# The attention output's column tiles hold token quarters in place of heads, and VectorE's block transposes replace TensorE's turns

## The chip, the cores and the metric

The kernel runs on one NeuronCore of a Trainium2 chip. The metric is the device time of one execution in microseconds (us), the median over the runs. Engines are named as in the profile: PE is TensorE's matmuls and PEld its weight loads, DVE is VectorE, ACT is ScalarE, POOL is GpSimd, and SP is SyncE, which here issues the DMAs.

## The reference

Two conditional attention layers follow each other on x of 8 sequences x 512 tokens x 512 features, all in float32. Only the second matters for the change; its core is:

```python
xn = layer_norm(x, norm_w, norm_b)
q = (xn @ q_w + q_b).reshape(Bx, Tx, H, -1)      # H = 16 heads of 32
k = (xn @ k_w + k_b).reshape(Bx, Tx, H, -1)
att = jnp.einsum('bnhl,bmhl->bnmh', q, k)
att = jax.nn.softmax(att + (1.0 - mask) * -1000000.0, axis=2)
v = ((xn @ v_w + v_b) * src_mask[:, :, None]).reshape(Bx, Tx, H, -1)
y = jnp.einsum('bnmh,bmhl->bnhl', att, v).reshape(Bx, Tx, Dx)
h = layer_norm(y, sb_norm_w, sb_norm_b) * (1.0 + scale) + shift
return x + silu(h) @ out_w + out_b
```

scale and shift come from a second input and are the same for all tokens of a sequence. The first layer has the same frame with linear attention in place of the softmax.

## The kernel before

**Stages.** First come the eight sequences of layer 0, up to about 550 us, then the attention layer until about 1400 us, then a tail. The attention of sequence b is cut into four units g = 0..3 of four heads each, n = 4b + g counts all 32. The rest of a sequence's work (norm, q, k and v of sequence b+1; norm, tanh and output product of sequence b-1) is woven into the units.

**Order.** `the_order` makes one list of steps and every engine walks through it, doing its own part of each step. `weave` merges tracks: `PLAN` gives for each track where in a unit it begins and ends, and `COST` how the steps of a track share that stretch. Nothing is sorted at run time. An engine that waits in a step holds up all that stands behind it in its list.

**One unit n.**
- S: 16 matmuls (PE L648) of the stacked keys `Ks` and queries `Qs`, 98 rows deep; DVE takes the row maximum of each (L1184). `nxt` (PE L656, ACT L891) puts the negative maxima as further rows into `Qs` of that unit.
- a: 16 matmuls (PE L665), the transposed scores less their maximum; ACT takes the exponential into `Pb` (L908). POOL (L1346) and, for few, DVE (L1213) add the four key tiles of `Pb` up, for the sums of the softmax.
- pv: PE L703. The output of the four heads of a unit lands in one PSUM bank `PV`: column tile j (32 partitions) holds head j, the 512 tokens are the columns, and four key tiles m add up. Two steps of two key tiles each.
- den: PE L681. Multiplies the sums by `sel`, a column of ones, into the bank `DEN`: column tile j is head j, row g of it the unit. It is issued ahead of the next unit's pv (in unit 0 ahead of the a matmuls).
- ae, tl: ACT copies `PV` to `yt` = `vt[1]` (L916), PE turns the four 128x128 blocks (`turn`, L487, `ps<-identr,vt`, since then tokens are the partitions) back into `PV`, and ACT copies that into its 128 columns of `yb` (L924). The turn and the copy stand in the next unit. For g = 0 (in unit 1) ACT first waits for `s_lo`, POOL's last read (L1324) of `yb` for the sequence before.
- tlx, once per sequence: ACT copies `DEN` to `yt` (L929), PE turns it, DVE takes the reciprocal into `rd` (L1230), DVE (L1237) and POOL (L1362) multiply two token tiles of `yb` each.

**What runs beside the units.** For sequence b-1: bn_stats of `yb` (DVE L1030), the norm (POOL L1270, ACT L755), PE's transposes of `yb`, tanh (ACT L858), DVE L1155 and L1158, which write the result into `yb` again, then `sTh` (ACT L865) and the rest `sTl` = `yb` - `sTh` (POOL L1324), and the output product o (PE L492 to L494). For sequence b+1: the products of v, k and q in three parts each (PE L492 to L494; high and low parts `xTh`, `xTl`), ACT L883 and DVE L1176, which split q and k into `sg_q`, `sg_k`.

**Loads.** SP stores `sg_q` and `sg_k` to DRAM (L1505, L1506) and loads them stacked into `Qs` and `Ks` (L1518), two units ahead; for units 0 and 1 the mask rows (L1523) go with them. `load_x` (L1375) brings the x of a later sequence into the buffer that held v, so it waits for the last pv of a sequence, and it stands in SP's list ahead of the loads of `Qs` and `Ks` for the unit after. `wr` loads (L1467) and output stores (L1473) move x by tiles of 128 tokens.

Of the kernel before, what the change touches and what calls it, by code (L numbers as in the profile page):

```python
# [18 lines left out]
NG = 4  # L19
# [15 lines left out]
    "tl": (0.2, 0.1, 0.9), "tlx": (1.0, 0.0, 0.4, 0.4, 0.4, 0.4),  # L35
# [217 lines left out]
def cond_two_layers(nc, A, out):  # L253
# [4 lines left out]
    with ctx:  # L258
# [23 lines left out]
        yt = vt[1]  # L282
# [12 lines left out]
        rd = cU[:].rearrange("p a b -> p (a b)").rearrange("p (t g j) -> p t g j", t=NT, g=NG)  # L295
# [6 lines left out]
        sel = sb("sel", [128, 36])  # L302
# [37 lines left out]
        for i in range(2):  # L340
# [137 lines left out]
        def _(e):  # L478
# [189 lines left out]
            def den(i, n):  # L668
                b, g = divmod(n, NG)
                pool, dve = ps_count(n, 3, 3)  # L670
                e.wait_ge(s["Ps_pool"], pool)
                if dve:
                    e.wait_ge(s["Ps_dve"], dve)
                if n == 0:
                    e.wait_ge(s["sel"], 2)
                    if bank_before["bank", 7] is not None:
                        e.wait_ge(*done(bank_before["bank", 7]))
                elif g == 0:
                    e.wait_ge(s["rd"], b)
                for j in range(4):  # L680
                    r = e.matmul(DEN[32 * j:32 * j + 32, :], sel[:, 4 - g:36 - g], p_buf(n, 0)[:, j, :],  # L681
                                 start=(g == 0), stop=(g == NG - 1))
                r.then_inc(s["den"], 1)

            def pv(i, n, first):
# [4 lines left out]
                for m in (first, first + 1):  # L690
# [27 lines left out]
            parts = {"m": m, "mb": mb, "tx": tx, "k": k, "v": v, "te": te, "q": q, "st": state, "y": y, "ty": ty, "o": o,  # L718
                     "qk": qk, "S": S, "nxt": nxt, "a": a, "pv": pv, "den": den, "tl": tl, "tlx": tlx}
# [5 lines left out]
        def _(e):  # L725
# [184 lines left out]
            def ae(i, n):  # L910
                if n:
                    e.wait_ge(s["y1_tr"], n)
                if n and n % NG == 0:
                    e.wait_ge(s["d1_tr"], n // NG)
                e.wait_ge(s["PV"], 4 * n + 4)
# [15 lines left out]
            parts = {"w": w, "nx": nx_, "ny": ny, "tx": tx, "k": k, "te": te, "v": v, "q": q, "sta": sta, "y": y, "ty": ty,  # L931
                     "early": early, "stacks": stacks, "qk": qk, "nxt": nxt, "a": a, "ae": ae, "tl": tl, "tlx": tlx}
# [5 lines left out]
        def _(e):  # L938
# [283 lines left out]

            def tlx(i, b):
                if i == 1:
                    if b:
                        e.wait_ge(s["y1_sc"], 4 * b)
                    else:
                        e.wait_ge(s["y_sc"], 64)
                    e.wait_ge(s["d1_tr"], b + 1)
                    e.reciprocal(rd.rearrange("p t g j -> p t j g"),  # L1230
                                 DEN[:].rearrange("p (t j l) -> p t j l", t=NT, j=4)[:, :, :, 0:4]).then_inc(s["rd"], 1)
                if i in (2, 4):
# [4 lines left out]
                    e.tensor_tensor(y3, y3, rd[:, t, :, :].rearrange("p g j -> p (g j)").unsqueeze(2).to_broadcast([128, H1, 32]),  # L1237
# [4 lines left out]
                     "y": y, "ty": ty, "o": o, "qk": qk, "S": S, "nxt": nxt, "a": a, "ae": ae, "tlx": tlx}  # L1242
# [5 lines left out]
        def _(e):  # L1248
            def prologue():
# [10 lines left out]
                e.memset(sel[:, 4:5], 1.0).then_inc(s["sel"], 1)  # L1260
# [95 lines left out]
            def tlx(i, b):  # L1356
                if i in (3, 5):
# [4 lines left out]
                    e.tensor_tensor(y3, y3, rd[:, t, :, :].rearrange("p g j -> p (g j)").unsqueeze(2).to_broadcast([128, H1, 32]),  # L1362
# [9 lines left out]
        def _(e):  # L1372
# [86 lines left out]
            def ty(i, x, c):  # L1459
                if i == 0 and c == 0:  # L1460
# [126 lines left out]
```

## Time and profile before

| | us |
|---|---|
| median of 2 runs | 1434.27 |
| lowest and highest | 1432.98, 1435.56 |
| profiled execution, its own time | 1437.03 |
| its span, first to last instruction | 1435.2 |
| mean granted TensorE clock, share of full | 0.983 |

The profile's times are those of the one profiled execution, counted from its first instruction; its own time is 1.8 us more than the span and 2.8 more than the median. One float32 matmul of the program is two pairs of a weight load and a matmul in the records (high and low part of the weights), so `L703 ... x16` is one step of two key tiles and four heads. PE's records overlap: a matmul of 512 columns has a duration of about 0.4 us though the next begins 0.23 us later, so what one costs is read from start to start. In the chain of waits the durations are from start to start.

### The profile page before, as it was taken

To read this page: it belongs to the slowest core of one execution; us is meant where nothing else is said; L and a number is where in the kernel's file an instruction comes from. 1 tells how busy PE (TensorE), PEld (TensorE's weight loads), DVE (VectorE), ACT (ScalarE), POOL (GpSimd) and SP (SyncE) were. 2 spreads that over 40 slices of the span, in tenths; PEclk is the share of its full clock that TensorE was granted. 3 is DMA by queue.
4 is the path that set the end of the run, shared out by engine and by line. 5 is a ranking of instruction groups with operands and counts; after the bars stand their busy time and mean duration, and the time that the engine had idled before them with its cause. 6 is when DMAs were issued, how large, how long until landed. Compare 5 with 4: busy or idle time off the path is not lost.

```text
span 1435.2 us, 20521 instructions
## 1 busy us (share of the span) xinstructions
PE 1350.1 (94%) x7040; PEld 974.1 (68%) x7040; DVE 1002.1 (70%) x1958; ACT 820.0 (57%) x1417; POOL 771.7 (54%) x692
## 2 busy tenths in 40 slices
PE   6899999999999899999999999999999999999985
PEld 4778888888888675565666666666665666666633
DVE  5787888878788786577657657657657657657554
ACT  4355455454455636557757756756756756756552
POOL 0323344233432524477577667667667757757752
PEclk9999999999999999999999999999999999999997
DMA  9021120211313177536436436435435534633610
GB/s 332 1 67 59 38 92 19 82 60 38 96 34 113 67 214 226 175 100 195 133 105 199 126 117 189 135 119 181 143 118 169 155 118 143 181 119 109 180 43 29
DMA packets 82888, 172.93 MB, mean 120 GB/s; under 512 B 7240, under 2 KB 7240, under 8 KB 82784
## 3 DMA queue, kind: packets, MB, share of 16 engines
q1 hardware_dynamic: 82784, 171.62, 39.0%
q8 instruction: 56, 0.92, 0.3%
q14 instruction: 48, 0.39, 0.1%
HBM read 104.45 MB, written 67.14 MB: 120 GB/s over the span
## 4 chain that ended last, share of the span: by engine, by line
PE 63%; DVE 13%; DMA 10%; ACT 6%; POOL 3%; issue 3%; SPq 2%; POOLq 0%; DVEq 0%; ACTq 0%
PE ps L492 12%; PE ps L494 12%; PE ps L493 11%; PE ps L648 6%; PE ps L703 6%; PE ps L665 5%; DMA Ks<-stack_scratch 5%; DVE cT L1184 5%; PE ps L487 4%; DMA Ks<-mask_scratch 3%; PE ps L681 2%; PE ps L580 1%; ACT xTh L769 1%; PE ps L601 1%; ACT ps L771 1%
## 5 line engine op out<-in xcount | busy, mean ns | idle before, releaser
L1346 POOL TENSOR_TENSOR Pb<-Pb 128x512 f32<-128x512 f32 x376 | 471.1, 1293 | 224.6 <-PE ps L703 224.6
L1184 DVE TENSOR_REDUCE cT<-ps 128x1 f32<-128x512 f32 x512 | 326.8, 684 | 120.1 <-PE ps L648 116.7
L908 ACT ACTIVATE Pb<-ps 128x512 f32<-128x512 f32 x512 | 288.1, 602 | 196.6 <-PE ps L665 181.2
L648 PE MATMUL ps<-Ks,Qs 98*128 98x512 f32 x512 | 192.1, 415 | 13.9 <-DMA Ks<-stack_scratch 7.0
L665 PE MATMUL ps<-Qs,Ks 106*128 106x512 f32 x512 | 197.7, 412 | 0.7 <-ACT Qs L891 0.4
L648 PEld LDWEIGHTS ps<-Ks,Qs 98*128 98x128 f32 x512 | 95.4, 189 | 78.5 <-issue 28.5
L665 PEld LDWEIGHTS ps<-Qs,Ks 106*128 106x128 f32 x512 | 95.5, 189 | 41.0 <-issue 14.3
L1298 POOL TENSOR_TENSOR vt<-vt,qmx 128x512 f32<-128x512 f32 x32 | 33.8, 1057 | 164.3 <-DVE qmx L1108 164.3
L1270 POOL TENSOR_TENSOR rs<-ve,mhalf 128x4 f32<-128x4 f32 x32 | 33.0, 1033 | 165.5 <-DVE ve L1016 115.6
L492 PE MATMUL ps<-Wh_o,sTh 128*128 128x512 f32 x256 | 107.7, 421 | 2.9 <-DVE sTl L1163 2.8
L492 PE MATMUL ps<-xTh,Wh_k 128*128 128x512 f32 x256 | 106.4, 416 | 2.5 <-DVE xTl L1043 1.4
L492 PE MATMUL ps<-Wh_v,xTh 128*128 128x512 f32 x256 | 103.3, 403 | 0.0
L494 PE MATMUL ps<-Wh_o,sTl 128*128 128x512 f32 x256 | 102.3, 400 | 0.0
L493 PE MATMUL ps<-Wl_o,sTh 128*128 128x512 f32 x256 | 101.7, 397 | 0.0
L494 PE MATMUL ps<-xTh,Wl_k 128*128 128x512 f32 x256 | 101.3, 396 | 0.0
L493 PE MATMUL ps<-xTl,Wh_k 128*128 128x512 f32 x256 | 100.9, 394 | 0.0
L494 PE MATMUL ps<-Wh_v,xTl 128*128 128x512 f32 x256 | 100.5, 393 | 0.0
L493 PE MATMUL ps<-Wl_v,xTh 128*128 128x512 f32 x256 | 100.2, 391 | 0.0
L1311 POOL TENSOR_TENSOR wr<-wr,boB 128x512 f32<-128x512 f32 x64 | 82.4, 1299 | 13.6 <-DMA wr<-in_x 13.6
L1170 DVE TENSOR_TENSOR wr<-ps,wr 128x512 f32<-128x512 f32 x64 | 44.0, 688 | 44.8 <-PE ps L494 33.1
L891 ACT CAST Qs<-ps 10x1024 fp32r<-10x1024 f32 x64 | 61.3, 1005 | 17.9 <-PE ps L656 17.2
L1043 DVE TENSOR_TENSOR xTl<-ps,xTh 128x512 fp32r<-128x512 f32 x64 | 44.0, 688 | 39.3 <-ACT ps L771 38.9
(175 smaller groups left out, 2935.9 us busy)
## 6 DMA issues: line engine op xcount, KB each, us to landing
Qs<-stack_scratch SPq DMA_DIRECT2D x32, 768.0 KB
Ks<-stack_scratch SPq DMA_DIRECT2D x32, 768.0 KB
stack_scratch<-sg_q SPq DMA_DIRECT2D x32, 512.0 KB, 2.7
stack_scratch<-sg_k SPq DMA_DIRECT2D x32, 512.0 KB, 2.6
wr<-in_x SPq DMA_DIRECT2D x32, 256.0 KB, 5.2
x_scratch<-wr SPq DMA_DIRECT2D x32, 256.0 KB, 2.0
stack_scratch<-sg_q SPq DMA_DIRECT2D x32, 256.0 KB, 3.0
stack_scratch<-sg_k SPq DMA_DIRECT2D x32, 256.0 KB, 3.3
```

Of the source, the lines that this page charges most:

```text
L487: r = e.transpose(bank[:, t * 128:(t + 1) * 128], src, ident)
L492: e.matmul(bank[:], lh(k), rh(k), start=(k == 0), stop=False)
L493: e.matmul(bank[:], lh(k), rl(k), start=False, stop=False)
L494: return e.matmul(bank[:], ll(k), rh(k), start=False, stop=(k == NC - 1))
L648: e.matmul(bank[:], Qs[par][0:RX, j, t * 128:(t + 1) * 128], Ks[par][0:RX, j, :], start=True, stop=True).then_inc(s["S"], 1)
L665: e.matmul(bank[:], Ks[par][0:RE, j, m * 128:(m + 1) * 128], Qs[par][0:RE, j, :], start=True, stop=True).then_inc(s["ST"], 1)
L703: r = e.matmul(PV[32 * j:32 * j + 32, :], xbuf(8 + b)[:, m, h * 32:(h + 1) * 32], pb[:, j, :], start=(m == 0), stop=(m == NT - 1))
L891: e.copy(Qs[n % 2][RM:RE, 2 * h:2 * h + 2, :], rows).then_inc(s["nxq"], 1)
L908: e.activation(p_buf(n, m)[:, j, :], ps[bank_of["a", n, m, j]][:], ACT.Exp).then_inc(s["P"], 1)
L1184: e.tensor_reduce(nx[:, n % 2, j, t, 0:1], ps[bank_of["S", n, j, t]][:], AX.X, ALU.max, negate=True).then_inc(s["S_max"], 1)
L1311: e.tensor_tensor(wr[t][:], wr[t][:], boB[:], ALU.add).then_inc(s["xb"], 1)
L1346: e.tensor_tensor(acc[:, j, :], acc[:, j, :], p_buf(n, m)[:, j, :], ALU.add).then_inc(s["Ps_pool"], 1)
```

## The change

PE's column tiles hold token quarters u (128 tokens each) instead of heads. In `PV`, partitions 32u to 32u+31 hold the 32 features of a head for quarter u, and head j has columns 128j to 128j+127. So each program matmul has 128 columns instead of 512, and there are 64 instead of 16 in a unit's pv. In `DEN` row h of each tile is head h (16 rows), the 128 columns are the quarter's tokens, all units adding into the same rows: 16 program matmuls per unit instead of 4.

A 32x32 block transpose on DVE (STREAM_TRANSPOSE in the order; every block of 32 partitions by 32 columns is turned in place) then gives rows of tokens: it reads `PV` and writes `yb` directly, once per unit (tl); and it reads the 128 columns of `DEN` and writes `dt`, a piece of `vt[1]` (tlx, i = 0), from which the reciprocal is taken. PE's turns of `PV` and `DEN`, ACT's three copies (L916, L924, L929) and their semaphores are gone. In row p of token tile t now stands token 128u + 32t + r with p = 32u + r, so the x and out tiles of layer 1 are loaded and stored by `token_tile`, rows of 2 KB as before. The wait for `s_lo` is now DVE's. `COST` of tl is one step and of tlx six with other shares, which moves neighbouring steps slightly.

```diff
-    "tl": (0.2, 0.1, 0.9), "tlx": (1.0, 0.0, 0.4, 0.4, 0.4, 0.4),
+    "tl": (0.3,), "tlx": (0.1, 0.3, 0.4, 0.4, 0.4, 0.4),
...
-        yt = vt[1]
+        dt = vt[1][:, 0:128]
...
-        rd = cU[:].rearrange("p a b -> p (a b)").rearrange("p (t g j) -> p t g j", t=NT, g=NG)
+        rd = cU[:].rearrange("p a b -> p (a b)").rearrange("p (t h) -> p t h", t=NT)
...
                 elif g == 0:
-                    e.wait_ge(s["rd"], b)
+                    e.wait_ge(s["dT"], b)
                 for j in range(4):
-                    r = e.matmul(DEN[32 * j:32 * j + 32, :], sel[:, 4 - g:36 - g], p_buf(n, 0)[:, j, :],
-                                 start=(g == 0), stop=(g == NG - 1))
+                    h = 4 * g + j
+                    for u in range(4):
+                        r = e.matmul(DEN[32 * u:32 * u + 32, 0:128], sel[:, H1 - 1 - h:H1 + 31 - h],
+                                     p_buf(n, 0)[:, j, 128 * u:128 * u + 128], start=(h == 0), stop=(h == H1 - 1))
                 r.then_inc(s["den"], 1)
...
                     for j in range(4):
                         h = 4 * g + j
-                        r = e.matmul(PV[32 * j:32 * j + 32, :], xbuf(8 + b)[:, m, h * 32:(h + 1) * 32], pb[:, j, :],
-                                     start=(m == 0), stop=(m == NT - 1))
+                        for u in range(4):
+                            r = e.matmul(PV[32 * u:32 * u + 32, 128 * j:128 * j + 128], xbuf(8 + b)[:, m, h * 32:(h + 1) * 32],
+                                         pb[:, j, 128 * u:128 * u + 128], start=(m == 0 and j == 0),
+                                         stop=(m == NT - 1 and j == 3))
                     r.then_inc(s["PV"], 1)
...
-            def tl(i, n):
-                b, g = divmod(n, NG)
-                if i == 1:
-                    e.wait_ge(s["yT"], n + 1)
-                    turn(PV, [yt[:, t * 128:(t + 1) * 128] for t in range(NT)]).then_inc(s["y1_tr"], 1)
-
-            def tlx(i, b):
-                if i == 1:
-                    e.wait_ge(s["dT"], b + 1)
-                    turn(DEN, [yt[:, t * 128:(t + 1) * 128] for t in range(NT)]).then_inc(s["d1_tr"], 1)
...
-            def ae(i, n):
...
-                e.copy(yt[:], PV[:]).then_inc(s["yT"], 1)
-
-            def tl(i, n):
-                if i == 2:
-                    b, g = divmod(n, NG)
-                    if g == 0:
-                        e.wait_ge(s["s_lo"], 4 * (8 + b))
-                    e.wait_ge(s["y1_tr"], n + 1)
-                    e.copy(yb[:, :, g * 128:(g + 1) * 128], t4(PV)).then_inc(s["y1"], 1)
-
-            def tlx(i, b):
-                if i == 0:
-                    e.wait_ge(s["den"], 4 * b + 4)
-                    e.copy(yt[:], DEN[:]).then_inc(s["dT"], 1)
...
+            def tl(i, n):
+
+                b, g = divmod(n, NG)
+                if g == 0:
+                    e.wait_ge(s["s_lo"], 4 * (8 + b))
+                e.wait_ge(s["PV"], 4 * n + 4)
+                e.transpose(yb[:, :, g * 128:(g + 1) * 128].rearrange("p t (j d) -> p j t d", j=4),
+                            PV[:].rearrange("p (j t r) -> p j t r", j=4, t=NT)).then_inc(s["y1"], 1)
+
             def tlx(i, b):
+                if i == 0:
+                    if b:
+                        e.wait_ge(s["rd"], b)
+                    e.wait_ge(s["den"], 4 * b + 4)
+                    e.transpose(dt, DEN[:, 0:128]).then_inc(s["dT"], 1)
                 if i == 1:
...
-                    e.wait_ge(s["d1_tr"], b + 1)
-                    e.reciprocal(rd.rearrange("p t g j -> p t j g"),
-                                 DEN[:].rearrange("p (t j l) -> p t j l", t=NT, j=4)[:, :, :, 0:4]).then_inc(s["rd"], 1)
+                    e.wait_ge(s["dT"], b + 1)
+                    e.reciprocal(rd, dt.rearrange("p (t h) -> p t h", t=NT)[:, :, 0:H1]).then_inc(s["rd"], 1)
...
+            def token_tile(a, x, t):
+
+                if x < 8:
+                    return a[x, t * 128:(t + 1) * 128, :]
+                return a[x % 8].rearrange("(u t r) d -> t u r d", u=4, t=NT)[t]
```

The first place where the order differs is in VectorE's list, in unit 1 of a sequence. L1155 and L1158 are steps of tanh of the sequence before, `sg_q` and `sg_k` the low parts of q and k, and `cT<-ps` the row maxima. Before:

```order
L1155 TENSOR_SCALAR ps<-ps,mod 128x512 [waits s_y_tanh]
L1158 SCALAR_TENSOR_TENSOR yb<-tb,ps 128x4x128 [waits s_y_u]
L1009 BN_STATS st<-xin 128x6 [waits s_l_x0]
L1011 BN_AGGR mv<-st 128x2 [waits s_x_st]
L1176 SCALAR_TENSOR_TENSOR sg_q<-ps,cols,sg_q 128x512 [waits s_q1_hi]
L1176 SCALAR_TENSOR_TENSOR sg_k<-ps,cols,sg_k 128x512 [waits s_k1_hi]
L1009 BN_STATS st<-xin 128x6 [waits s_l_x0]
L1011 BN_AGGR mv<-st 128x2 [waits s_x_st]
L1184 TENSOR_REDUCE cT<-ps 128x1 [waits s_S,s_nx_lo]
L1184 TENSOR_REDUCE cT<-ps 128x1 [waits s_S] x2
```

The same place now:

```order
L1127 TENSOR_SCALAR ps<-ps,mod 128x512 [waits s_y_tanh]
L1130 SCALAR_TENSOR_TENSOR yb<-tb,ps 128x4x128 [waits s_y_u]
L981 BN_STATS st<-xin 128x6 [waits s_l_x0]
L983 BN_AGGR mv<-st 128x2 [waits s_x_st]
L1201 STREAM_TRANSPOSE yb<-ps 128x4x4x32 [waits s_PV,s_s_lo]
L1148 SCALAR_TENSOR_TENSOR sg_q<-ps,cols,sg_q 128x512 [waits s_q1_hi]
L1148 SCALAR_TENSOR_TENSOR sg_k<-ps,cols,sg_k 128x512 [waits s_k1_hi]
L981 BN_STATS st<-xin 128x6 [waits s_l_x0]
L983 BN_AGGR mv<-st 128x2 [waits s_x_st]
L1156 TENSOR_REDUCE cT<-ps 128x1 [waits s_S,s_nx_lo]
L1156 TENSOR_REDUCE cT<-ps 128x1 [waits s_S] x2
```

The transpose of unit 0's output, with its waits for `PV` and `s_lo`, stands ahead of `sg_q`, `sg_k` and all that follows.

The second place is PE's list at the start of unit 0, behind the v products (`Wh_v,xTl`). Before:

```order
L494 MATMUL ps<-Wh_v,xTl 128x512
L487 MATMUL ps<-identr,vt 128x128 [waits s_yT]
L487 MATMUL ps<-identr,vt 128x128 x3
L681 MATMUL ps<-Pb,sel 32x512 [waits s_Ps_pool]
L681 MATMUL ps<-Pb,sel 32x512 x3
L665 MATMUL ps<-Qs,Ks 128x512 [waits s_nxq,s_P]
L665 MATMUL ps<-Qs,Ks 128x512 [waits s_S_max]
L487 MATMUL ps<-identr,vt 128x128 [waits s_dT]
L487 MATMUL ps<-identr,vt 128x128 x3
L665 MATMUL ps<-Qs,Ks 128x512 [waits s_nxq,s_P]
```

The same place now:

```order
L494 MATMUL ps<-Wh_v,xTl 128x512
L683 MATMUL ps<-Pb,sel 32x128 [waits s_Ps_pool]
L683 MATMUL ps<-Pb,sel 32x128 x15
L665 MATMUL ps<-Qs,Ks 128x512 [waits s_nxq,s_P]
L665 MATMUL ps<-Qs,Ks 128x512 [waits s_S_max]
L665 MATMUL ps<-Qs,Ks 128x512 [waits s_nxq,s_P]
```

Both turns, with their waits for ACT's copies (`s_yT`, `s_dT`), are gone, and DEN's matmuls are 16 of 128 columns.

## Rows read from the trace of the kernel before

**Rows 1.** The page's busy times (share of the span) and instructions by engine.

```profile
PE 1350.1 (94%) x7040; PEld 974.1 (68%) x7040; DVE 1002.1 (70%) x1958; ACT 820.0 (57%) x1417; POOL 771.7 (54%) x692
```

**Rows 2.** Windows view, one period: length, busy time (count) by engine, clock, DMA share, GB/s.

```profile
869.00:978.00 109.00, 105.27 (x549) 69.80 (x548) 70.78 (x128) 71.42 (x118) 75.43 (x62) 1.00 0.49 146
```

**Rows 3.** S matmuls (L648), 650 to 1305: PE idle ahead, until what (us, times).

```profile
  DMA Ks<-stack_scratch: 5.1, 6
  DMA Ks<-mask_scratch: 1.8, 4
```

**Rows 4.** Chain of waits, pieces: start, us to the next, what.

```profile
650.85 10.89 DMA Ks<-mask_scratch
...
864.60 0.23 PE ps L494
...
866.75 0.37 SPq L1375
...
868.23 10.74 DMA Ks<-mask_scratch
...
1195.67 10.87 DMA Ks<-mask_scratch
```

**Rows 5.** Timeline of PE, unit 1 of a sequence: start, us, engine, line, tiles, count.

```profile
1010.76 0.48 PE L648 MATMUL ps<-Ks,Qs 98*128 98x512 f32 x1 [0.39 <-DMA Ks<-stack_scratch]
1011.07 0.60 PE L487 MATMUL ps<-identr,vt 128*128 128x128 f32 x4
1011.43 0.47 PE L665 MATMUL ps<-Qs,Ks 106*128 106x512 f32 x1
```

**Rows 6.** Timeline of PE, unit 0 of the same sequence.

```profile
977.62 0.60 PE L487 MATMUL ps<-identr,vt 128*128 128x128 f32 x4
978.15 1.06 PE L681 MATMUL ps<-Pb,sel 128*32 128x512 f32 x8
979.14 0.73 PE L665 MATMUL ps<-Qs,Ks 106*128 106x512 f32 x2
980.26 0.66 PE L487 MATMUL ps<-identr,vt 128*128 128x128 f32 x4 [0.38 <-ACT vt L929]
980.67 1.17 PE L665 MATMUL ps<-Qs,Ks 106*128 106x512 f32 x4
```

**Rows 7.** Timelines of VectorE and GpSimd, unit 1 of the same sequence.

```profile
1008.88 0.75 DVE L1176 SCALAR_TENSOR_TENSOR sg_q<-ps,cols,sg_q 128x512 fp32r<-128x512 f32 x1 [1.95 <-ACT sg_q L883]
1009.54 0.74 DVE L1176 SCALAR_TENSOR_TENSOR sg_k<-ps,cols,sg_k 128x512 fp32r<-128x512 f32 x1
1010.81 1.29 POOL L1324 TENSOR_TENSOR sTl<-yb,sTh 128x512 fp32r<-128x512 f32 x1
```

**Rows 8.** The page's costliest groups: count, busy, mean ns, idle before and its end.

```profile
L1184 DVE TENSOR_REDUCE cT<-ps 128x1 f32<-128x512 f32 x512 | 326.8, 684 | 120.1 <-PE ps L648 116.7
```

**Rows 9.** Timeline of PE, DEN and one PV step in unit 1.

```profile
1014.65 1.06 PE L681 MATMUL ps<-Pb,sel 128*32 128x512 f32 x8
1015.54 1.90 PE L703 MATMUL ps<-Pb,xin 128*32 128x512 f32 x16
1017.37 0.50 PE L648 MATMUL ps<-Ks,Qs 98*128 98x512 f32 x1
```

**Rows 10.** Windows view of L703 alone, from 10 ns behind its start: PE, PEld (count).

```profile
1015.55:1015.56 0.01, 0.01 (x4) 0.01 (x4) 1.00 0.00 0
```

**Rows 11.** Timelines of VectorE and PE, the tail.

```profile
1388.93 7.48 DVE L1213 TENSOR_TENSOR Pb<-Pb 128x512 f32<-128x512 f32 x8 [9.24 <-ACT Pb L908]
1397.27 1.94 PE L681 MATMUL ps<-Pb,sel 128*32 128x512 f32 x8
1400.67 0.56 DVE L1230 RECIPROCAL cU<-ps 128x64 f32<-128x64 f32 x1 [4.26 <-PE ps L487]
```

**Rows 12.** Timeline of PE and windows view (as in rows 2) behind the longest stall.

```profile
1340.25 0.47 PE L648 MATMUL ps<-Ks,Qs 98*128 98x512 f32 x1 [1.98 <-DMA Ks<-stack_scratch]
...
1341.60:1345.00 3.40, 3.40 (x10) 2.63 (x9) 1.38 (x2) 1.57 (x3) 0.00 (x0) 0.50 0.30 113
```

More of the change, by code:

```diff
@@ L300, in cond_two_layers @@
         nm = sb("nm", [128, 2, NT])
-        sel = sb("sel", [128, 36])
+        sel = sb("sel", [128, 31 + H1])
         nx = cT[:].rearrange("p a b -> p (a b)").rearrange("p (n j t s) -> p n j t s", n=2, j=4, s=2)
@@ L362, in cond_two_layers @@
             "S", "S_max", "nx_set", "nx_hi", "nx_neg", "nx_lo", "nx_tr", "nxq", "ST", "P", "PV", "Ps_pool", "Ps_dve",
-            "yT", "y1_tr", "y1", "den", "dT", "d1_tr", "rd", "y1_sc")}
+            "y1", "den", "dT", "rd", "y1_sc")}
         def xbuf(x):
@@ L908, in a @@
                 e.activation(p_buf(n, m)[:, j, :], ps[bank_of["a", n, m, j]][:], ACT.Exp).then_inc(s["P"], 1)
-            def ae(i, n):
[L911 to L915, printed above, removed]
-                e.copy(yt[:], PV[:]).then_inc(s["yT"], 1)
-            def tl(i, n):
-                if i == 2:
-                    b, g = divmod(n, NG)
-                    if g == 0:
-                        e.wait_ge(s["s_lo"], 4 * (8 + b))
-                    e.wait_ge(s["y1_tr"], n + 1)
-                    e.copy(yb[:, :, g * 128:(g + 1) * 128], t4(PV)).then_inc(s["y1"], 1)
-            def tlx(i, b):
-                if i == 0:
-                    e.wait_ge(s["den"], 4 * b + 4)
-                    e.copy(yt[:], DEN[:]).then_inc(s["dT"], 1)
             parts = {"w": w, "nx": nx_, "ny": ny, "tx": tx, "k": k, "te": te, "v": v, "q": q, "sta": sta, "y": y, "ty": ty,
-                     "early": early, "stacks": stacks, "qk": qk, "nxt": nxt, "a": a, "ae": ae, "tl": tl, "tlx": tlx}
+                     "early": early, "stacks": stacks, "qk": qk, "nxt": nxt, "a": a}
             for p, i in order:
@@ L1236, in tlx @@
                     y3 = yb[:, t, :].rearrange("p (h l) -> p h l", h=H1)
-                    e.tensor_tensor(y3, y3, rd[:, t, :, :].rearrange("p g j -> p (g j)").unsqueeze(2).to_broadcast([128, H1, 32]),
+                    e.tensor_tensor(y3, y3, rd[:, t, :].unsqueeze(2).to_broadcast([128, H1, 32]),
                                     ALU.mult).then_inc(s["y1_sc"], 1)
@@ L1241, in _ @@
             parts = {"early": early, "w": w, "mb": mb, "nx": nx_, "ny": ny, "tx": tx, "k": k, "te": te, "v": v, "q": q, "qn": qn, "sta": sta,
-                     "y": y, "ty": ty, "o": o, "qk": qk, "S": S, "nxt": nxt, "a": a, "ae": ae, "tlx": tlx}
+                     "y": y, "ty": ty, "o": o, "qk": qk, "S": S, "nxt": nxt, "a": a, "ae": ae, "tl": tl, "tlx": tlx}
             for p, i in order:
@@ L1259, in prologue @@
                 e.wait_ge(s["sel"], 1)
-                e.memset(sel[:, 4:5], 1.0).then_inc(s["sel"], 1)
+                e.memset(sel[:, H1 - 1:H1], 1.0).then_inc(s["sel"], 1)
                 e.wait_ge(s["sel"], 2)
@@ L1361, in tlx @@
                     y3 = yb[:, t, :].rearrange("p (h l) -> p h l", h=H1)
-                    e.tensor_tensor(y3, y3, rd[:, t, :, :].rearrange("p g j -> p (g j)").unsqueeze(2).to_broadcast([128, H1, 32]),
+                    e.tensor_tensor(y3, y3, rd[:, t, :].unsqueeze(2).to_broadcast([128, H1, 32]),
                                     ALU.mult).then_inc(s["y1_sc"], 1)
@@ L1466, in ty @@
                             e.wait_ge(s[f"st{t}"], 16 * x)
-                        e.dma_start(wr[t][:], src[x % 8, t * 128:(t + 1) * 128, :]).then_inc(s[f"l_xr{t}"], 16)
+                        e.dma_start(wr[t][:], token_tile(src, x, t)).then_inc(s[f"l_xr{t}"], 16)
             def o(i, x, t):
@@ L1472, in o @@
                     dst = x1d if x < 8 else out
-                    e.dma_start(dst[x % 8, t * 128:(t + 1) * 128, :], wr[t][:]).then_inc(s[f"st{t}"], 16)
+                    e.dma_start(token_tile(dst, x, t), wr[t][:]).then_inc(s[f"st{t}"], 16)
             def ahead(i):
```

2 lines of the change are left out of this document (1 added, 1 removed).

## The prediction

> **What bounds the kernel now.** I began with the busy shares [rows 1]: TensorE (PE) is busy 94% of the span, VectorE 70%, ScalarE 57%, GpSimd 54%. The first question is whether this holds where the change sits. The windows view of one whole sequence of the attention layer [rows 2] gives 105.27 us of matmul in 109.00 us at full granted clock (1.00 is the 2.4 GHz level), so some 3.7 us per sequence are idle, and what the change takes off TensorE can count only where no other wait ends later. The list of S matmuls in the six middle sequences [rows 3] says what those waits are: PE stands idle ahead of an S 6 times for a stacked load (5.1 us) and 4 times for the mask load (1.8 us). The chain of waits shows the second kind in full [rows 4]: PV matmuls, then SP's issue of load_x (L1375, it waits for the last PV since it overwrites the v buffer), then 10.74 us of flight of the load behind it, then S. The chain runs through this in four sequences, the first at 650.85 and the last at 1195.67. The work in between is not on the path. So there are three kinds of places: unit 0 of a sequence (between the PV that frees the buffer and the first S of the new stack) is bound by a transfer; unit 1 begins with an S that waits for a stacked load; units 2 and 3 and the tail are bound by PE.
>
> **What goes from PE.** Each turn of PV costs PE four short matmuls and an entry. In unit 1 the S at 1010.76 and the matmul at 1011.43 lie 0.67 apart [rows 5] where two neighbours are 0.23 apart (the PE step of the chain in [rows 4]): 0.44. In units 2 and 3 I take 0.36 each, the turn's own stretch 1011.07 to 1011.43. In unit 0 both turns stand [rows 6]: from 977.62 to 978.15 for PV, 0.53; and from 979.14 to 980.67, 1.53, less two matmuls of 0.23 and 0.1 for leaving the block ahead: 0.97 for DEN, of which 0.38 is a wait for ScalarE's copy. Sum: 0.44 + 0.72 + 0.53 + 0.97 = 2.66 per sequence, and for seven and a half sequences 19.9 us. The ScalarE copies (0.59 each) go too; that engine has room.
>
> **What of that counts.** The 1.50 of unit 0 lie between the PV that lets load_x go and the mask load's landing: these are taken up by a longer idle time ahead of the S. In units 2 and 3 the 0.72 count in full. Per sequence, then, 0.72 on the path, and 0.44 in unit 1, if nothing else is late there.
>
> **The new wait in unit 1.** Something else is late. VectorE now writes yb itself, so it takes over the wait for s_lo: yb of the sequence before must have been read for the last time by GpSimd (fourth L1324, 1010.81 + 1.29 = 1012.10 in this sequence [rows 7]). The order places the transpose of g = 0 ahead of sg_q and sg_k, which today run at 1008.88 and 1009.54. Behind it stand both of these, two bn_stats and the reduces of S. PE's S of this unit writes the bank that sg_q reads, and the a behind it the bank that sg_k reads. In the six middle sequences the fourth L1324 ends, against the S, between 0.17 and 1.34 us later, 0.76 in the mean (in the one shown 1012.10 against 1010.76, the largest). I estimate that it comes 0.9 earlier: GpSimd's adds start behind its multiply, which waits for the reciprocal, and of the 0.97 above nearly all lies ahead of that. So S starts at 0.76 - 0.9 + transpose 0.69 + sg_q 0.66 (the distance of the two rows) + 0.1 to start = 1.3 us later than now, and a 0.66 behind it, which is the 0.67 of today. The unit ends 1.3 later: the 0.44 removed are eaten, and 1.3 put on top. Bounds: with an s_lo that isn't late at all 0.44 are gained; with no earlier s_lo and a transpose of 1.3 it is 2.8.
>
> **The transpose on VectorE** is in no row. The nearest are reads of 128x512 from PSUM: the row maximum L1184 at 0.684 [rows 8] and, at the other end, two passes of it, 1.37; below, a move can't be quicker than the 0.56 of the reciprocal of 64 numbers [rows 11]. I take 0.69, near the first row. In units 2 and 3 it lies in VectorE's idle 35% [rows 2]; without that cover it would cost PE its own length.
>
> **The finer matmuls.** PE's columns stay the same, 4 tiles by 128 for 4 by 512, but the starts are fourfold: the two PV blocks of a unit go from 16 to 64 matmul records each, DEN's from 8 to 32. Today a block of 16 takes 1.83 [rows 9] (1015.54 to 1017.37), four rounds of four tiles at 0.43, and DEN's two rounds 0.89. Sixteen rounds of 0.107 have the same sum; a round costs some 3 ns over its columns (0.430 against 1024 cycles at 2.4 GHz, 0.427), so 12 more rounds are 0.036 per block, and with DEN 0.09 per unit, 0.28 per sequence where it counts. This rests on PE starting a pair of weight load and matmul each 27 ns. In the windows view four are in flight 20 ns after a round's start [rows 10], so short bursts go that fast; sixty-four in a row no row shows.
>
> **Ends.** In sequences 2, 4 and 7 the chain passes through the scaling of yb, where 0.2 to 0.3 is to be had: -0.6. Sequence 0 has no late s_lo ahead of it: -0.5. The last has more room in its loads: -1.0. In the tail [rows 11] VectorE's adds end at 1388.93 + 7.48 = 1396.41; DEN is held up till 1397.27 by the turn, ends some 1.94 later, then come copy, turn and reciprocal, done at 1401.23. After the change DEN starts near 1396.5, ends at 1398.4, then a transpose of 128 columns (0.3) and the reciprocal (0.56): 1399.4, so -1.8.
>
> **Sum** against the profiled execution's own 1437.03 (span 1435.2): six sequences of 1.3 - 0.72 + 0.28 = 0.86 are +5.2; with -0.6, -0.5, -1.0 and -1.8 it is +1.3, 1438.3. That execution lies 2.76 above the median of the runs, 1434.27, so in the runs' frame 1435.5; I say 1435.4. Its own range is 1428 to 1444.
>
> **Rival 1, the savings come in full.** If the transfers of unit 0 land earlier with less waiting about, and GpSimd's last L1324 is done before VectorE gets to the transpose, all of it counts: -19.9 - 1.8 + 2.8 (0.09 for each of 31 units) = -18.9, 1415.4. For it: PE is the bound by share. Against: 6.9 us of idle time in 10 waits for loads [rows 3], whose start hangs on PV and not on the turns.
>
> **Rival 2, the wait grows.** The transpose takes 1.3 and s_lo is no earlier: 1.5 more in each of seven sequences, +10.5. And a longer idle stretch can drop the clock: ahead of 1340.25 PE sat idle for 1.98, and from 1341.6 to 1345.0 the granted clock was 0.50, the 1.2 GHz level [rows 12], so half of 3.4 is lost, about 1.6 to 1.7. The stalls of unit 1 would reach that length in two sequences: +3. Together 1449; with the clock lost in all seven 1457.
>
> **Rival 3, slower: PE can't start them fast enough.** One mechanism: the matmuls of the column tiles are too short for PE's rate of starts. The turns' pairs of 128 columns start 0.10 apart, four in 0.41 [rows 6] (980.26 to 980.67). If only two such pairs overlap, a PV block takes 64 x 0.05 = 3.2 for 1.83 and DEN 1.6 for 0.89: +1.4 x 64 + 0.7 x 32 = +112, 1547; with none overlapping about +370. It decides from 35 ns a pair on (64 x 0.035 = 2.24, +0.41 a block, +0.2 a DEN: +32). For it: eight engine instructions per 107 ns are asked for without a pause, and the trace has nothing of the kind for 1.8 us on end. Against: the four starts of each round today lie within 20 ns [rows 10].
> The Trainium skill bears on this in "TensorE: Matmul & The Clock Gate", section "Wait — 56ns, not 53.3ns?": matmuls never start closer than about 25 ns, and with hardware decode off the sequencer spends about 62 ns on each. By the second figure, as an estimate, a block would take 64 x 62 ns = 4.0 and DEN 2.0, some +170 us, near 1605; by the first it stays at 27 ns and nothing is lost. The starts of today's rounds [rows 10] lie closer than both figures, which speaks against the 62 here.
>
> **Chances.** Forecast 0.60, rival 1 0.13, rival 2 0.13, rival 3 0.14. Faster or slower by over 2%, which is about what a measurement of this kernel can tell from no change, begins at 1405.6 and 1463.0: no sum of the savings reaches the first (0.02 for what I don't see), rival 3 alone the second (0.14), the rest is within (0.84). The range reaches from rival 1 to the upper end of rival 2: 1415 to 1458.
>
> **What would show it.** Right: a PV block still takes 1.85 to 1.9; the idle time ahead of the first S of a sequence grows from 0.5 to about 2 us; the VectorE transpose takes 0.7 and in unit 1 waits for GpSimd's L1324 (or a late stamp near it); sg_q lies some 2 us later against the S; a sequence stays at 109 to 110 us; the reciprocal of the tail ends near 1.8 earlier against the adds. Wrong: a PV block above 2.2 (rival 3), a period near 106.5 (rival 1), a transpose of 1.3 or stretches with a clock of 0.50 in several sequences (rival 2).

## The result, and the profile after

The changed kernel takes 1514.47 us (median of 2 runs, 1513.19 to 1515.75) against 1434.27: a ratio of 1.056, interval 1.050 to 1.062, so 80 us slower, where 1435.4 and a range of 1415 to 1458 had been forecast. The profiled execution ran for 1515.75 us.

The busy times come first, then a windows view of one period of the attention layer; it answers to [rows 1] and [rows 2].

```profile
PE 1357.0 (90%) x10720; PEld 1076.5 (71%) x10720; DVE 1024.7 (68%) x1998; ACT 783.3 (52%) x1345; POOL 771.8 (51%) x692
```

```profile
906.79:1027.95 121.16, 107.76 (x1008) 83.51 (x1009) 74.11 (x132) 66.95 (x109) 75.42 (x63) 0.94 0.45 132
```

PE has only 7 us more of busy time in the whole span, for 3680 more records. But a period lasts 121.16 where the same one, from S to S of unit 0, lasted 108.8 (879.11 to 987.93 in the timeline of before), PE's idle time in it is 13.4 instead of 3.6, and the mean clock is 0.94 for 1.00. So the loss isn't in the matmuls themselves. Where PE waits, the list of S matmuls says (idle time ahead of L648 from 650 to 1400, by what ended it: us, times), against [rows 3]:

```profile
  DMA Ks<-stack_scratch: 51.7, 6
  DMA Ks<-mask_scratch: 12.3, 6
```

51.7 us in six waits, 8.6 each, where there were 5.1. The timelines of SP, POOL, VectorE and PE show one of them, and two lines of the windows view what the DMA engines did meanwhile (as in [rows 2], the last two figures are DMA share and GB/s):

```profile
1037.43 2.99 SPq L1458 DMA_DIRECT2D wr<-x_scratch  x4
1040.52 3.02 SPq L1509 DMA_DIRECT2D Qs<-stack_scratch  x1
1043.59 1.87 SPq L1509 DMA_DIRECT2D Ks<-stack_scratch  x1
```

```profile
1052.05 1.26 POOL L1296 TENSOR_TENSOR wr<-wr,boB 128x512 f32<-128x512 f32 x1 [1.57 <-DMA wr<-x_scratch]
1053.27 1.26 POOL L1309 TENSOR_TENSOR sTl<-yb,sTh 128x512 fp32r<-128x512 f32 x1
```

```profile
1054.57 0.72 DVE L1201 STREAM_TRANSPOSE yb<-ps 128x512 f32<-128x512 f32 x1 [7.90 <-POOL sTl L1309]
```

```profile
1049.65 0.39 PE L665 MATMUL ps<-Qs,Ks 106*128 106x512 f32 x1
1058.43 0.77 PE L648 MATMUL ps<-Ks,Qs 98*128 98x512 f32 x1 [8.39 <-DMA Ks<-stack_scratch]
1058.99 0.63 PE L665 MATMUL ps<-Qs,Ks 106*128 106x512 f32 x1
1059.42 0.63 PE L492 MATMUL ps<-Wh_o,sTh 128*128 128x512 f32 x1
```

```profile
1042.00:1044.00 2.00, 2.00 (x12) 1.67 (x11) 1.93 (x4) 1.38 (x3) 1.29 (x1) 1.00 0.26 101
1052.00:1056.00 4.00, 0.00 (x0) 0.00 (x0) 1.43 (x3) 0.00 (x0) 3.70 (x3) 0.77 0.26 97
```

SP needs 3.02 us to issue the load of `Qs`, 0.38 before the change. While the four `wr` loads run, and again in the last stretch before the stack load lands, only 0.26 of the 16 DMA engines' time is busy, at 101 and 97 GB/s. That is 4 engines. In the windows view of before, the stretch in which the same loads run, together with the end of `sg_k`'s store, has all of them:

```profile
997.60:1001.00 3.40, 3.40 (x30) 1.79 (x30) 3.37 (x6) 1.68 (x3) 3.40 (x4) 1.00 0.98 319
```

In the changed kernel four engines move the x tiles that `token_tile` takes in four pieces, and their part of the stack load comes behind these: POOL has the third x tile only at 1052.05, and the stack load lands at 1058.30 in the chain of waits. With the x tiles `s_lo` is late too, and VectorE waits 7.90 us for it. And once PE goes on, its steps are 0.43 apart (1058.99 to 1059.42) where 0.23 was usual: half clock.

What the prediction had sized is otherwise as forecast. The timeline of PE has a PV block of 64 records at 1.88 from start to start (1037.76 to 1039.64):

```profile
1037.76 1.95 PE L706 MATMUL ps<-Pb,xin 128*32 128x128 f32 x64
1039.64 1.53 PE L487 MATMUL ps<-identr,yb 128*128 128x128 f32 x12
```

VectorE's 32 transposes last 0.698 to 0.718. In the tail (timelines of PE and VectorE) the adds end at 1465.33 + 6.97 = 1472.30, and the reciprocal at 1474.63, 2.3 later where it was 4.8 [rows 11]. Of these 2.5 us, 0.9 is the clock: DEN takes 1.08 at full clock here, and 1.94 in before, where the windows view has 0.50 from 1397.30 to 1399.20. The rows after the change:

```profile
1465.33 6.97 DVE L1185 TENSOR_TENSOR Pb<-Pb 128x512 f32<-128x512 f32 x8 [9.06 <-ACT Pb L901]
...
1472.45 1.08 PE L683 MATMUL ps<-Pb,sel 128*32 128x128 f32 x32 [2.54 <-DVE Pb L1185]
...
1474.08 0.55 DVE L1216 RECIPROCAL cU<-vt 128x64 f32<-128x64 f32 x1
```

### The profile page after: what moved, and what is told of

It reads as the page before. It is cut to its first block, busy times and chain, and to the rows that moved or that the text cites. A ratio compares the mean times of both kernels' runs of the same rounds, so it can differ in the third digit from the quotient of the medians.

```text
span 1514.0 us, 27825 instructions
## 1 busy us (share of the span) xinstructions
PE 1357.0 (90%) x10720; PEld 1076.5 (71%) x10720; DVE 1024.7 (68%) x1998; ACT 783.3 (52%) x1345; POOL 771.8 (51%) x692
## 4 chain that ended last, share of the span: by engine, by line
PE 61%; DMA 13%; DVE 13%; ACT 5%; SPq 3%; issue 3%; POOL 2%; POOLq 0%; DVEq 0%; ACTq 0%
PE ps L492 12%; PE ps L493 11%; PE ps L494 11%; DMA Ks<-stack_scratch 7%; PE ps L648 7%; PE ps L706 6%; PE ps L665 5%; DMA Ks<-mask_scratch 4%; DVE cT L1156 4%; PE ps L487 4%; PE ps L683 2%; SPq L1509 2%; PE ps L601 1%; PE ps L580 1%; SPq L1458 1%
## 5 line engine op out<-in xcount | busy, mean ns | idle before, releaser
L648 PE MATMUL ps<-Ks,Qs 98*128 98x512 f32 x512 | 200.2, 435 | 79.0 <-DMA Ks<-stack_scratch 60.2
L648 PEld LDWEIGHTS ps<-Ks,Qs 98*128 98x128 f32 x512 | 100.9, 200 | 130.7 <-issue 83.6
L665 PEld LDWEIGHTS ps<-Qs,Ks 106*128 106x128 f32 x512 | 99.9, 197 | 35.6 <-DVE cT L1156 5.9
```

Of the source, the lines that this page charges most:

```text
L648: e.matmul(bank[:], Qs[par][0:RX, j, t * 128:(t + 1) * 128], Ks[par][0:RX, j, :], start=True, stop=True).then_inc(s["S"], 1)
L665: e.matmul(bank[:], Ks[par][0:RE, j, m * 128:(m + 1) * 128], Qs[par][0:RE, j, :], start=True, stop=True).then_inc(s["ST"], 1)
```

## The experiments

The runs were made on several chips, each beside its own runs of the kernel before, which took 1437 to 1439 us there; so runs from different chips are compared by their ratios.

**1 to 4: which part costs?** Four kernels: the changed one with `token_tile` undone in both places, in the loads alone and in the stores alone, and the kernel before with `token_tile` put in. All four leave rows of the residual or of the output in another place than the reference has them.

```diff
-                        e.dma_start(wr[t][:], token_tile(src, x, t)).then_inc(s[f"l_xr{t}"], 16)
+                        e.dma_start(wr[t][:], src[x % 8, t * 128:(t + 1) * 128, :]).then_inc(s[f"l_xr{t}"], 16)
...
-                    e.dma_start(token_tile(dst, x, t), wr[t][:]).then_inc(s[f"st{t}"], 16)
+                    e.dma_start(dst[x % 8, t * 128:(t + 1) * 128, :], wr[t][:]).then_inc(s[f"st{t}"], 16)
```

> The changed kernel, but with x and out tiles of layer 1 taken as 128 neighbouring tokens as before (which leaves the rows of the residual and of the output in another place than the reference has them). Theory A (the permuted tiles of token_tile run on about 4 of 16 DMA engines and hold up the stack loads behind them in SP's queue): the long stalls of unit 1 (8.4 to 9.6 us) go, the sequence period falls from about 123 to 109 to 110 us, and the time is 1430 to 1440. Theory B (VectorE's wait for s_lo ahead of sg_q and sg_k is the stall's cause, the loads come second): the stall of unit 1 stays above 5 us and the time above 1480.

> The kernel before with nothing changed but the permuted x and out tiles of layer 1 (rows of residual and output in another place). Theory A: most of the 80 us appear here, 1495 to 1515, with the wr loads' packets on about 4 engines at once. Theory B: no transposes on VectorE, no new wait, so 1434 to 1440.

> The changed kernel with the loads of x by neighbouring tokens and the output stores still permuted (the residual's rows don't belong to the output's). Theory A: the loads stand directly ahead of the stack loads, so they make most of it: 1435 to 1450. If the stores were as bad as the loads: around 1470 to 1480. Theory B: 1500 and above.

> The changed kernel with permuted loads and the output stores by neighbouring tokens. Theory A: 1495 to 1512, nearly all of the loss is still there. If the stores were as bad as the loads: around 1470 to 1480. Theory B: 1500 and above, so this run tells A and B apart only together with the run of plain loads.

| kernel | us | ratio to before (interval) |
|---|---|---|
| changed, both plain | 1470.57 | 1.022 (1.019 to 1.026) |
| before, both permuted | 1513.88 | 1.052 (1.049 to 1.054) |
| changed, plain loads | 1472.48 | 1.023 (1.019 to 1.027) |
| changed, plain stores | 1511.31 | 1.050 (1.046 to 1.054) |

Permuted tiles put 75 us on the kernel before. The changed kernel tells loads from stores: permuted loads alone cost it 41 us (run 4 against run 1), permuted stores alone 2, which the intervals don't tell from zero (run 3 against run 1). But with both plain it is still 32 us too slow: theory A is right on the loads and wrong in saying that nothing else is left. And 75 and 32 are more than the 80 of the change, so the two overlap; run 16 is on that. The timelines of VectorE and PE in the run with plain rows, unit 1 of one sequence:

```profile
1029.62 0.72 DVE L1201 STREAM_TRANSPOSE yb<-ps 128x512 f32<-128x512 f32 x1 [4.65 <-POOL sTl L1309]
1030.26 0.71 DVE L1148 SCALAR_TENSOR_TENSOR sg_q<-ps,cols,sg_q 128x512 fp32r<-128x512 f32 x1
```

```profile
1027.96 0.39 PE L665 MATMUL ps<-Qs,Ks 106*128 106x512 f32 x1
1031.02 0.49 PE L648 MATMUL ps<-Ks,Qs 98*128 98x512 f32 x1 [2.67 <-DVE sg_q L1148]
1031.68 0.50 PE L665 MATMUL ps<-Qs,Ks 106*128 106x512 f32 x1 [0.16 <-DVE sg_k L1148]
```

This is the mechanism that the prediction had for unit 1, step by step: POOL's last L1309, the transpose, `sg_q`, S. And PE's idle time ahead of S, by releaser (us, times), has its price, 2.7 each, and beside it the mask load of unit 0 at 2.1 each:

```profile
  DVE sg_q L1148: 18.9, 7
  DMA Ks<-mask_scratch: 12.6, 6
```

Behind the stall the clock falls, as a windows view of the same run shows:

```profile
1032.50:1035.90 3.40, 3.40 (x10) 2.62 (x9) 2.67 (x5) 0.99 (x2) 0.00 (x0) 0.50 1.00 387
```

**5 and 6: repair both.** For plain tiles the quarter u must hold the tokens 128t + 32u + r. Then, on top, the transpose of unit 0's output goes behind `sg_q` and `sg_k` on VectorE, by one number of `PLAN`.

```diff
+            def quarter(cols, u):
+                return cols.rearrange("p (t v r) -> p v t r", t=NT, v=4)[:, u]
...
-                                     p_buf(n, 0)[:, j, 128 * u:128 * u + 128], start=(h == 0), stop=(h == H1 - 1))
+                                     quarter(p_buf(n, 0)[:, j, :], u), start=(h == 0), stop=(h == H1 - 1))
```

```diff
-    "tl": (None, (0.012, 0.917), (0, 0.654), (0, 0.723)),
+    "tl": (None, (0.25, 0.917), (0, 0.654), (0, 0.723)),
```

> The changed kernel with x and out tiles of 128 neighbouring tokens, and quarter u of the columns holding the tokens 128t + 32u + r, which TensorE reads as four runs of 32 columns. Theory A (runs of 32 columns are read at full rate): the same 1470 as the run of plain rows, a PV block at 1.88 us. Rival: runs of 128 bytes slow the moving read, a PV block at 2.5 us or more and the time at 1510 or more.

> The same with VectorE's transpose of unit 0's output moved in the order behind sg_q, sg_k and three row maxima (one number of PLAN). Theory A (the rest of the loss is the transpose's wait for s_lo, ahead of sg_q and sg_k, and the half clock that each stall brings): the stall of unit 1 falls from 3.05 to about 0.8 us, the granted clock stays at 1.00 in the middle of the attention layer, and the time is 1428 to 1440. Rival (the loss sits in the column tiles or in the stall of 2.4 us in unit 0): 1460 and above.

Strided: 1471.17, ratio 1.022 (1.018 to 1.026), the same as with plain rows, so TensorE reads four runs of 32 columns at no cost: DEN takes 0.90 and a PV block 1.86 in the timeline of that run's PE.

```profile
1034.74 1.08 PE L686 MATMUL ps<-Pb,sel 128*32 128x128 f32 x32
1035.64 1.93 PE L709 MATMUL ps<-Pb,xin 128*32 128x128 f32 x64
1037.50 0.50 PE L648 MATMUL ps<-Ks,Qs 98*128 98x512 f32 x1
```

Transpose moved: 1447.83, ratio 1.0057 (1.003 to 1.008). The wait on `sg_q` is gone, and the edit is worth 23 us, but the time lies above the 1428 to 1440 expected. PE's idle time ahead of S in this run:

```profile
  DMA Ks<-mask_scratch: 12.4, 6
  DMA Ks<-stack_scratch: 9.7, 7
```

**7 and 8: load_x behind the stack loads**, in that kernel and in the one before (SP issues it in the step after).

```diff
-            def ae(i, n):
+            def tl(i, n):
                 b, g = divmod(n, NG)
-                if g == NG - 1 and b + 2 < B:
+                if i == 0 and g == NG - 1 and b + 2 < B:
```

> The same, and SP issues load_x behind the stack loads of unit 0 and no longer ahead of them. Theory A (what the change takes off TensorE in unit 0 is eaten by the wait for the mask load, which starts behind load_x): the stall of unit 0 of 2.4 us falls below 0.5, and the time lies 8 to 18 us below the run before, at 1415 to 1425. Rival (the loads are bound by their own length of 9 us and by the stores): less than 4 us.

> The kernel before with that one edit of load_x, to tell it from the change. Its stalls of unit 0 sum to some 3 us and it ran through the mask load in four sequences, so 1430 to 1436: 0 to 4 us less than before. If the load of x was worth more than this view shows, below 1428.

1446.22, ratio 1.0045 (1.002 to 1.007), against 1.0057 (1.003 to 1.008) without it: 1.6 us, which the intervals don't tell from zero, where 8 to 18 were expected. And 1434.90, ratio 0.998 (0.996 to 1.001), for the kernel before: nothing that can be told from zero. The stall of unit 0 did go, from 12.4 us to none in the list, but another took its place:

```profile
  ACT Pb L904: 12.3, 13
  DMA Ks<-stack_scratch: 10.0, 6
```

S now waits for a bank that ScalarE's exp (L904) frees. What holds exp up is seen in ScalarE's timeline of run 11, which has this stall too: it stands behind the norm of the sequence before (L751), which waits 4.30 for POOL.

```profile
1095.57 0.81 ACT L751 ACTIVATE yb<-yb,nm,rs 128x512 f32<-128x512 f32 x1 [4.30 <-POOL nm L1261]
1096.29 0.67 ACT L879 ACTIVATE sg_q<-ps,cols 128x512 fp32r<-128x512 f32 x1
1096.86 0.58 ACT L904 ACTIVATE Pb<-ps 128x512 f32<-128x512 f32 x1
```

That norm hangs on DEN, reciprocal and scaling, not on how soon PE gets to S: in the timelines of that run the reciprocal begins at 1086.85, the scaling of `yb` ends at 1090.49 and the statistics of it at 1093.81, and POOL's L1261 ends at 1095.53. So the idle time ahead of S stayed what it was.

**9: is it the clock?** In the kernel of run 6 each wait for a stack load is filled with idle matmuls, whose result the first S overwrites.

```diff
                 if j == 0 and t == 0:
+                    for _ in range({1: 9, 2: 6}.get(n % NG, 0) if n > 4 else 0):
+                        e.matmul(bank[:], Wh["q"][:, 0, 0:128], Wh["q"][:, 0, :], start=True, stop=True)
                     e.wait_ge(s[f"stack{par}"], stack_count(n))
```

> The kernel with strided quarters and the transpose behind sg_k, plus idle work on TensorE: ahead of its wait for the stack load it issues 9 (unit 0) or 6 (unit 1) matmuls of 512 columns into the bank that the first S will overwrite; the result isn't used. Theory C (the 9 us that are left over the kernel before are mostly half clock behind stalls of 1.6 to 2.6 us, 6 windows of 3.4 us against 1): the granted clock stays at 1.00 there and the time falls by 5 to 10 us, to 1438 to 1443. Rival (the stalls themselves cost it, the clock little): no less than 1446, or more, since the fillers can run over the landing.

1438.63, ratio 1.0009 (0.999 to 1.003), for 1.0057: 7 us won by work that does nothing. The stalls are about as long as before, only TensorE is busy in them: from the last matmul ahead of them to S it is 2.43 us in run 6 (1104.20 to 1106.63) and 2.29 here (1094.93 to 1097.22). PE's timeline of run 6, ahead of a first S of unit 0, and the windows view behind it; then the same place in this run:

```profile
1106.63 0.47 PE L648 MATMUL ps<-Ks,Qs 98*128 98x512 f32 x1 [2.03 <-DMA Ks<-mask_scratch]
```

```profile
1107.90:1111.30 3.40, 3.40 (x10) 2.63 (x9) 3.17 (x6) 2.75 (x5) 3.40 (x4) 0.50 0.54 214
```

```profile
1095.16 2.23 PE L645 MATMUL ps<-Wh_q 128*128 128x512 f32 x9
1097.22 0.40 PE L650 MATMUL ps<-Ks,Qs 98*128 98x512 f32 x1
```

```profile
1098.50:1101.90 3.40, 3.40 (x16) 2.60 (x15) 3.40 (x6) 3.34 (x6) 3.40 (x4) 1.00 0.57 223
```

Between 600 and 1390 us run 6 has six stretches of 3.4 us at 0.50, run 5 thirteen, and the run with fillers one, at 1147.4, behind a stall of 1.40 us elsewhere. The Trainium skill says in "TensorE: Matmul & The Clock Gate", section "What's actually happening", that a gate sets the clock by how busy TensorE has been; the runs agree, 0.50 and 1.00 in the two rows.

**10 to 12: the wr loads ahead of their time.** The four `wr` loads are issued behind `sg_q`'s store and no longer between `sg_k`'s and the stack load, in the kernel of run 6, with load_x behind as well, and in the kernel before.

```diff
+                    if which == 0 and n % NG == 2 and n > NG:
+                        load_wr(7 + n // NG)
```

> The same kernel without fillers, with the loads of x tiles into wr issued behind the store of sg_q in unit 0, no longer behind sg_k's, directly ahead of the stack load of unit 1. Theory C2 (the stall of unit 1 is set by what stands ahead of its stack load on SP and the DMA engines: four loads, 2.5 us of issue): its stall goes from about 2.1 to below 0.5 and the time falls by 10 to 16 us (seven stalls and their half clocks), to 1432 to 1438. Rival (it is set by the store of sg_k and the 9 us of the load itself): under 3 us.

> The same with load_x behind the stack loads too. Theory C: both DMA stalls are gone, what is left is the wait of S for a bank that ScalarE's exp frees late (1.7 us behind the norm of the sequence before); 1425 to 1433, less than the kernel before. Rival (the chain from DEN through reciprocal, norm and tanh takes its place): no less than the run without this edit.

> The kernel before with that one edit of the wr loads, to tell it from the change. Its stalls of unit 1 are 0.78 us in the mean, so 3 to 7 us less: 1431 to 1436. If nothing changes, the stall was bound by the load alone.

| kernel | us | ratio to before (interval) |
|---|---|---|
| run 6, wr early | 1435.59 | 0.9985 (0.997 to 1.000) |
| the same, load_x behind | 1431.12 | 0.9966 (0.995 to 0.998) |
| before, wr early | 1427.32 | 0.9928 (0.991 to 0.995) |

All but the last are as expected; that one is better than its 1431 to 1436. The stall of unit 1 is gone in all three: it was set by what stood ahead of its stack load on SP and the DMA engines. The edit gives the kernel before 10 us, as much as it gives run 6 (1.0057 to 0.9985). That is more than the 5.1 us of stalls that the forecast went by, and the trace of before has most of the rest: over the whole attention layer there are seven such stalls with 7.0 us, and the longest, 1.98, is followed by 3.4 us at 0.50 [rows 12], 1.7 lost. In run 12 neither these stalls nor a stretch at 0.50 is left between 600 and 1380 us.

**13: filler in unit 0 alone**, on the kernel of run 10.

> The kernel with strided quarters, the transpose behind sg_k and the early wr loads, with 9 idle matmuls of 512 columns ahead of the first S of unit 0 only. Theory C (the stall of 2.5 us there costs nothing itself, the half clock behind it 1.6 us each time): 1425 to 1430, 6 to 10 us below the run without them and level with the kernel before with early wr loads (1427). Rival (the clock is not what is left): 1434 and above.

1429.22, ratio 0.9932 (0.991 to 0.996): 8 us below the run without the fillers, inside the forecast. The clock in the middle is 1.00 and a period 107.87 (S at 1094.72 and 1202.59 of its timeline). Level with the kernel before with early `wr` loads, which has no fillers: its interval and that one's overlap nearly wholly.

**14 and 15: why four engines?** The kernel before, permuted tiles, with the outer dimension of the pattern 16 or 8 in place of 4 (rows of 2 KB throughout).

```diff
-                return a[x % 8].rearrange("(u t r) d -> t u r d", u=4, t=NT)[t]
+                return a[x % 8].rearrange("(u t r) d -> t u r d", u=16, t=NT)[t]
```

> The kernel before with permuted x and out tiles of layer 1 whose outer dimension is 16 (16 pieces of 8 rows of 2 KB; rows of residual and output in another place). Theory D (a transfer goes to as many DMA engines as its outer dimension has steps): all 16 engines work and the time is that of the kernel before, 1434 to 1442. Rival (rows that don't follow each other in memory are slow in themselves): 1500 and above, as with 4 pieces.

> The same with an outer dimension of 8 (8 pieces of 16 rows). Theory D: about 8 packets at once, a wr load takes half as long as with 4; a third or less of the 75 us is left, 1440 to 1465. Rival: 1500 and above.

1445.53, ratio 1.004 (1.002 to 1.006), and 1478.91, ratio 1.028 (1.025 to 1.031). With 4 it was 1.052. The windows views of stretches in which the `wr` loads run, for outer dimensions of 4, 8 and 16 in turn:

```profile
1034.00:1036.00 2.00, 1.61 (x10) 1.43 (x11) 1.93 (x5) 1.35 (x3) 2.00 (x3) 1.00 0.25 95
```

```profile
1016.60:1018.00 1.40, 0.91 (x10) 0.70 (x7) 1.32 (x5) 1.40 (x3) 1.40 (x2) 1.00 0.48 167
```

```profile
1007.00:1009.00 2.00, 2.00 (x22) 0.86 (x15) 1.97 (x5) 0.88 (x2) 2.00 (x2) 1.00 0.94 289
```

A DMA share of 0.25 and 0.48 of 16 engines is 4 and 8. The 0.94 is nearly all of them, but the end of `sg_k`'s store runs in that stretch too, so it doesn't count the engines of the `wr` loads by itself; that these land a median 4.5 us after their issue, and 3.8 in before, fits. The Trainium skill has the rule in "DMA: Bandwidth & Descriptors", section "Why a DMA increments its semaphore by 16 and not by 1": the number of engines is the largest up to 16 that divides the slowest dimension of both patterns. The shares of runs 2 and 15 agree with it, and so does the time of run 14. Both expected times were too low: with 8 it was to be 1440 to 1465, and half the engines left 40 of 75 us; with 16 it was to be 1434 to 1442, and 6 us are left, beside 4.5 us more of waiting for stack loads than in before (11.5 in seven for 7.0).

**16: do the two costs add?** The changed kernel as it is, with the transpose moved as in run 6.

> The changed kernel as it is (outer dimension 4) with the transpose of unit 0's output moved behind sg_q, sg_k and three row maxima, nothing else. Theory (in unit 1 the S waits for both, the later one being the stack load; the wait for s_lo is hidden under it): 0 to 6 us less than the changed kernel, 1506 to 1514. Rival (the two add up, 23 us as between the runs with plain rows): 1488 to 1495.

1514.37, ratio 1.052 (1.049 to 1.055). No gain; with plain rows the same edit gave 23. Its idle time ahead of S shows why:

```profile
  DMA Ks<-stack_scratch: 50.8, 6
  DMA Ks<-mask_scratch: 12.3, 6
```

As long as the stack load lands 8 us late, the late `sg_q` beside it costs nothing.

## Why the prediction was wrong

**The step that failed is one the prediction doesn't contain.** It priced the matmuls, turns, copies and the new wait, and gave the tiles that `token_tile` loads and stores no term: rows of 2 KB as before, taken for the same transfer. That is an edit costed at nothing without naming what covers it. Run 2 puts it at 75 us on the kernel before, runs 1, 3 and 4 put it in the loads (41 us on top of what else the change costs, and 2 for the stores), in the place where the prediction's own reading had found that PE waits for a stacked load. No row of before shows a transfer with an outer dimension of four, but the rule of the Trainium skill that runs 2, 14 and 15 bear out speaks of just that, and the prediction weighed another page and not this one. As an estimate, the four tiles are 1.05 MB: at 97 GB/s 10.8 us, at the 319 of before 3.3, so 7.5 more per sequence ahead of the very load that PE waits for. The stall grew by 7.7 (8.6 for 0.85). In run 2 PE waits 59.3 us in seven such stalls for 7.0 in before: 52 of the 75 us. Its trace has most of the rest: behind each of the first six the clock stays at 0.50 for another 3.2 to 6.3 us after S has begun, 30 us in all, half of them lost.

**PE can start the short matmuls.** Rival 3, to which the chance of "slower" had been given, didn't happen: a PV block takes 1.88, as worked out (1.83 + 0.04). The sign that it named (a block above 2.2) is absent. The result is on its side of 2% for another reason; that 0.14 stood on "slower" was luck.

**The transpose** takes 0.70 to 0.72, for 0.69, and the tail gained 2.5 where 1.8 was forecast; the forecast had kept DEN's 1.94, which was a time at half clock.

**Unit 0 took its savings back**, as said: the stall ahead of its first S rose to 2.1 us (12.3 in 6), where "about 2" stood, and removing it (run 7) moved the wait to ScalarE's exp.

**The new wait in unit 1** was the right mechanism, mis-sized. The sum had S 1.3 later than now; in the run with plain rows PE waits 2.7 in each sequence where the stack load had let it wait 0.85 (5.1 in 6), so 1.85 later. In the one sequence that was read, `s_lo` came only some 0.5 earlier than today against PE and not 0.9 (in that run PE's last a begins at 1027.96 and the transpose, released by `s_lo`, at 1029.62: 1.66 later; in before s_lo ended at 1012.10, 2.12 behind the a of 1009.98). In time it was 32 us in all for the changed kernel with plain rows against the 1.3 forecast, of which 23 are gone once the transpose is moved. So the forecast would have missed without the DMA's fault too: run 1's 1470.57 lies above the range's 1458. And less than half of the 23 is the wait itself: PE's idle time for `sg_q` or a stack load ahead of S falls from 19.0 to 9.7 us between runs 5 and 6, while the stretches at 0.50 between 600 and 1390 us fall from thirteen to six, 1.7 us lost in each, 12 in all.

**The clock** was rival 2's, at 0.13 and with a price of 3 us. It is the second mis-sized term: stalls of 2 us and more now stand in unit 0 and unit 1 of every sequence, and behind many of them 3.4 us run at 0.50, 1.7 lost each time. Of the 9 us that were left in run 6, 7 went with the fillers. Rival 2 named the clock, but not its size: with plain rows the changed kernel lies 32 us over before, above even the 23 of its worst case (1457), and by stalls and clock, not by a slow transpose.

**What stays open:** what the change would be worth with the chain behind DEN shortened too, and what the shifted steps of `COST` do by themselves, which no run separates. With both faults repaired, early `wr` loads and fillers in unit 0, it is worth nothing beside the kernel before with early `wr` loads alone (0.9932 against 0.9928); without the fillers it is 8 us slower (0.9985).

## What to carry to other kernels

When a change alters the shape of a DMA's address pattern, look at how many steps its outermost dimension has, even if the contiguous run stays the same, and permute on the side of a matmul's moving read, where it was free, before permuting in memory. Where work is taken off the bounding engine, ask at each wait what ends second; what is removed ahead of a transfer comes back as idle time, and behind idle times of some 2 us the clock was here halved for 3.4 us, longer than they lasted. Two late things that meet at one instruction don't add up: take away the later one first, or a test of the other shows nothing.

## What the runs showed of the hardware

- DMAs of 128 rows of 2 KB kept 4 of 16 engines busy when their pattern's outermost dimension was 4 (share 0.25 at 95 GB/s), and 8 when it was 8 (0.48 at 167). With 16 the share was 0.94 at 289 GB/s, a store's end included.
- Four tiles of 32 columns take 64 pairs of weight load and matmul of 128 columns in 1.88 us, 29 ns a pair, and 32 pairs in 0.90; four runs of 32 columns are read as fast as one of 128.
- Behind a stall of 2.03 us (run 6, S at 1106.63) TensorE ran 1.3 us at full rate and then 3.4 us at the 1.2 GHz level; with idle matmuls in the stall it stayed at 2.4. Such a stretch also stood behind stalls of 1.40 us (run 9) and 1.57 us (run 11).
- A 128x512 float32 block transpose from PSUM took 0.71 us on VectorE, as a row maximum does (0.684).
- SP's issue of one load took 3.02 us in place of 0.38 while four transfers on four engines each were under way; in run 2, 2.75.
